# A six-layer decoder on one core: keys and values of the last attention moved into the experts' stage, the fp8 layer moved into the last attention's round

## The reference

```
x = x + L0_attn (layernorm(x))        # self attention, 16 heads of 64, rotary, causal
x = x + L0_xattn(layernorm(x), ctx)   # cross attention, 16 heads of 32, causal
x = x + L0_ffn  (layernorm(x))        # 32 experts, each takes its 8 best tokens
x = x + L1_attn (layernorm(x))        # q * sum(k * v), q and k of unit length
x = x + L1_xattn(layernorm(x), ctx)   # cross attention, 16 heads of 32, biases
x = x + L1_ffn  (layernorm(x))        # x and weight rounded to e4m3, product, bias
```

## Time and profile before

| | us |
|---|---|
| median of 3 runs (3672.01 to 3676.06) | 3674.29 |
| the profiled execution | 3670.53 |
| its span, first to last instruction | 3668.7 |
| mean granted TensorE clock | 0.926 of full |

### The profile page before, as it was taken

One profiled execution on the slowest core, in us unless ns is written; L12 is line 12 of the kernel. 1 busy time (PEld: TensorE's weight loads), 2 busy tenths in 40 slices (PEclk: granted clock), 3 DMA queues, 4 the chain that ended last, 5 costly groups with the idle time before them and its releaser, 6 DMA issues. The chain is left out here.

```text
span 3668.7 us, 71550 instructions
## 1 busy us (share of the span) xinstructions
PE 3132.1 (85%) x23760; PEld 2321.1 (63%) x23768; DVE 2103.6 (57%) x5235; ACT 1382.7 (38%) x4549; POOL 1312.0 (36%) x1964
## 2 busy tenths in 40 slices
PE   5999999999987999998575666659998899999935
PEld 5888888888865878786321111116776688888822
DVE  6666766667646787886500000016665667666667
ACT  4434434444434555554200000011111566666611
POOL 2544535445433444443100000002222455555537
PEclk9999999999998999999688877779999899999976
DMA  3001000000002211111699999971112111121123
GB/s 124 18 17 34 17 34 17 21 31 17 29 18 88 69 46 57 58 47 51 263 424 424 428 428 426 428 317 59 63 69 80 61 62 46 46 69 46 34 84 132
DMA packets 123955, 438.33 MB, mean 119 GB/s; under 512 B 11056, under 2 KB 30768, under 8 KB 103376
## 3 DMA queue, kind: packets, MB, share of 16 engines
q1 hardware_dynamic: 119792, 433.27, 30.4%
q10 hardware_dynamic: 4096, 4.20, 0.3%
HBM read 390.78 MB, written 46.66 MB: 119 GB/s over the span
## 5 line engine op out<-in xcount | busy, mean ns | idle before, releaser
L405 POOL TENSOR_TENSOR cross_prob<-cross_prob,cross_rsum 128x256 f32<-128x256 f32 (+1 forms) x1024 | 561.4, 576 | 626.5 <-DVE cross_rsum L780 624.9
L643 ACT ACTIVATE cross_prob<-cross_S,cross_neg_max 128x256 f32<-128x256 f32 (+1 forms) x1024 | 446.7, 455 | 93.6 <-DVE cross_neg_max L772 75.2
L405 POOL TENSOR_TENSOR self_prob<-self_prob,self_rsum 128x128 f32<-128x128 f32 (+1 forms) x512 | 285.3, 583 | 243.4 <-DVE self_rsum L780 243.3
L549 PE MATMUL cross_T<-cross_ident,cross_prob 128*128 128x128 f32 x1792 | 294.2, 281 | 25.3 <-ACT cross_probT L650 13.0
L643 ACT ACTIVATE self_prob<-self_S,self_neg_max 128x128 f32<-128x128 f32 (+1 forms) x512 | 212.0, 425 | 202.3 <-DVE self_neg_max L772 202.2
L1164 PE MATMUL experts_H<-moe_w,experts_tok 128*32 128x512 f32 x1024 | 164.9, 802 | 132.8 <-DMA moe_b<-in_L_ffn_w 126.9
L549 PEld LDWEIGHTS cross_T<-cross_ident,cross_prob 128*128 128x128 f32 x1792 | 203.6, 141 | 116.2 <-issue 43.2
L399 POOL TENSOR_TENSOR self_QK_T<-self_QK_T,self_turned 128x512 f32<-128x512 f32 x128 | 164.4, 1284 | 308.4 <-DVE self_QK_T L737 308.3
L785 DVE COPY cross_probT<-cross_T 128x384 f32<-128x384 f32 (+1 forms) x256 | 158.7, 620 | 150.8 <-PE cross_T L549 150.3
L650 ACT ACTIVATE cross_probT<-cross_T 128x384 f32<-128x384 f32 (+1 forms) x256 | 139.8, 546 | 279.2 <-PE cross_T L549 278.2
L1224 DVE COPY experts_hidT<-experts_T 128x512 f32<-128x512 f32 x32 | 22.1, 692 | 371.5 <-PE experts_T L1175 371.5
(11 more groups left out here) (252 smaller groups left out, 9109.0 us busy)
## 6 DMA issues: line engine op xcount, KB each, us to landing
moe_w<-in_L_ffn_w SPq DMA_DIRECT2D x64, 4096.0 KB, 34.7
cross_x_t<-x SPq DMA_DIRECT2D x32, 512.0 KB, 5.5
cross_c_t<-in_ctx SPq DMA_DIRECT2D x32, 512.0 KB, 6.4
cross_res<-x SPq DMA_DIRECT2D x32, 512.0 KB, 3.6
x<-cross_res SPq DMA_DIRECT2D x32, 512.0 KB, 2.8
self_x_t<-in_x SPq DMA_DIRECT2D x16, 512.0 KB, 3.6
self_res<-in_x SPq DMA_DIRECT2D x16, 512.0 KB, 3.6
x<-self_res SPq DMA_DIRECT2D x16, 512.0 KB, 2.8
```

The costliest lines, as they stand in the source:

```text
L405: ins = pool.tensor_tensor(pr, pr, rsum[:, h, t:t + 1].to_broadcast([P, KQ[t]]), ALU.mult)
L549: mm = pe.transpose(TP[:, o:o + P], prob[:, h % NP, SOFF[t] + k * P:SOFF[t] + (k + 1) * P], ident[:, :])
L643: ins = act.activation(prob[:, h % NP, SOFF[t]:SOFF[t] + KQ[t]], SC[h % G][:, SOFF[t]:SOFF[t] + KQ[t]], ACT.Exp, bias=neg_max[:, h, t:t + ...
```

## The change

Four things:

1. **K and V of the last attention move into experts.** In route, SP loads Wk and Wv in eight blocks of 128 rows and ACT and DVE split them beside the routing. In the experts' loop a turn (two experts) also takes one batch: SP loads its context, ACT and DVE split it, PE computes K in two halves and V in two halves, placed after hidden and after output, DVE copies them out (K with its bias), and ACT stores them to `keys_d` and `values_d` in DRAM, 512 KB each. The expert's bias row b1 is loaded as `[4, 512]` instead of `[1, 2048]`, and its product uses a constant `rows` loaded from DRAM instead of a row of ones made by POOL.
2. **One last phase** (`last_phase`) takes the place of cross1 and fp8. It loads K and V of each batch in 4 + 4 pieces, computes Q only, and carries the fp8 layer of the last batch in the same round: F (transposes of the quantised x) and G (products) on PE, fstats, fapply and G on DVE, F on ACT, frstd, fbias and fout on POOL. It has orders of its own.
3. **The fp8 weight** is rounded in norm, five of ten DVE steps in each of the last two batches, and goes through DRAM (512 KB).
4. **Prologues.** In the attention phases each projection waits for its own weight (`weights_for(w, c, n)`) and not for all; the splits of the later weights come after X1, and in self0 part of them after K0. In self0, where V, prob and QK_T serve as staging, the first writes to them wait for the last piece staged there (`staged`).

```diff
     "last": {
         "PE":   "Q2 T15- S1 PV3- T0 Q3 T1 O0- X0+ T2 S2 X1+ T3 O1- T4 Q0+ T5 S3 T6 Q1+ T7 PV0 T8 F0- F1- T9 PV1 T10 S0+ T11 G0- "
                 "T12 G1- T13 PV2 T14"
         "DVE":  "max3 take14- inv1 inv2 z2- stats+ max4 max5 take0 z3- max6 max7 apply+ inv3 inv4 O0- take2 X0+ inv5 max8 max9 "
                 "inv6 X1+ max10 inv7 max11 inv8 inv9 O1- take4 fstats- inv10 max12 take6 max13 fapply- max14 take8 z0 inv11 "
                 "max15 inv12 inv13 inv14 take10 max0+ max1+ max2+ take12 z1 inv15 inv0+ G0- G1-"
         "POOL": "rstd+ norm2 norm3 norm4 norm5 norm6 norm7 norm8 norm9 frstd- res norm10 norm11 norm12 norm13 norm14 fbias- "
                 "norm15 norm0+ fout- norm1+"
...
-            def weights_for(n):
+            def weights_for(w, c, n):
                 if isinstance(n, int) and n == 0:
-                    pe.wait_ge(w_lo, len(PIECES))
+                    pe.wait_ge(w_lo, PIECES.index((w, c)) + 1)
...
-            high_pieces(len(PIECES) - 2)
-            if bq is not None:
-                act.wait_ge(scaled, 1)
-            act.wait_ge(const_in, 16 * N_CONST)
+            high_pieces(1)
...
+                def load_rows(i):
+                    if i >= 3:
+                        sp.wait_ge(kv_lo, i - 2)
+                    sp.dma_start(kv_stage[:, i % 3, :], (wk, wv)[i // KD][i % KD * P:(i % KD + 1) * P, :]).then_inc(kv_in[i], 16)
...
             def _(sp):
+                sp.dma_start(rows[:, :, :], consts["rows"]).then_inc(rows_in, 16)
+                sp.dma_start(bk_c[:, :], bk).then_inc(bk_in, 16)
+                sp.dma_start(c_t[:, :, :], ctxT[0].rearrange("(k p) s -> p k s", p=P)).then_inc(c_in, 16)
                 with sp.Fori(1, E // 2) as i:
+                    sp.wait_ge(c_lo, 2 * i)
+                    sp.dma_start(c_t[:, :, :], ctxT[i].rearrange("(k p) s -> p k s", p=P)).then_inc(c_in, 16)
...
                 with pe.Fori(0, E // 2) as i:
-                    for s in range(2):
-                        hidden(2 * i + s, i, s)
-                        output(2 * i + s, i, s)
+                    hidden(2 * i, i, 0)
+                    pe.wait_ge(c_lo, 2 * i + 2)
+                    keys(i, 0)
+                    output(2 * i, i, 0)
+                    keys(i, 1)
+                    hidden(2 * i + 1, i, 1)
+                    values(i, 0)
+                    output(2 * i + 1, i, 1)
+                    values(i, 1)
...
+                        if s == 0:
+                            act.wait_ge(kv_ok, 4 * i + 4)
+                            act.dma_start(keys_d[bass.ds(i, 1)].rearrange("o g p s -> p (o g) s"), k_sb[:, :, :]).then_inc(k_stored, 16)
+                        else:
+                            act.wait_ge(kv_ok, 4 * i + 6)
+                            act.dma_start(values_d[:, bass.ds(i, 1)].rearrange("g o p t c -> p (g o) t c"), v_sb[:, :, :, :]).then_inc(v_stored, 16)
...
+                def keys_out(i, half):
+                    dve.wait_ge(kv_full, 4 * i + half + 2)
+                    dve.wait_ge(k_stored, 16 * i + 16)
+                    for j in range(2):
+                        g = 2 * half + j
+                        ins = dve.tensor_scalar(k_sb[:, g, :], KV[half][:, j * S:(j + 1) * S], bk_c[:, g:g + 1], None, ALU.add)
+                    ins.then_inc(kv_ok, 1)
...
             def body(n, i, s, last):
                 for u, (which, t) in enumerate(ORDER):
+                    if isinstance(n, int) and u < 5:
+                        quantise(u + 5 * s)
                     dve.wait_ge(p_full, NU * n + u + 1)
```

More of the change, by code:

```diff
@@ L1233, in norm_attention_phase @@
+                tokens(0, 0)
+                with dve.Fori(0, E // 2 - 1) as i:
+                    for s in range(2):
+                        expert(i, s, False)
+                for s in range(2):
+                    expert(E // 2 - 1, s, s == 1)
+def norm_attention_phase(nc, n_batch, x_in, x_out, consts, sel_d, out_d, w2, wq, bq, wk, bk, wv, bv, weight, w8_d):
     E, Q = out_d.shape[2], out_d.shape[1]
@@ new lines, in output @@
+            def output(key, n):
+                t = key[1]
+                pe.wait_ge(z_ok, n * NG + NG)
+                out = bank_for(key, n)
+                if isinstance(n, int) and n == 0:
+                    pe.wait_ge(w_lo, 2)
+                mm = split_products(pe, out[:, :], [((zTs[0][:, k, t * P:(t + 1) * P], zTs[1][:, k, t * P:(t + 1) * P]),
+                                                     (wos[0][:, k, :], wos[1][:, k, :])) for k in range(NG)])
+                full(mm, key, n)
@@ new lines, in linear_transposes @@
+            def linear_transposes(key, n):
+                pe.wait_ge(fl, NF * n + NF)
+                if isinstance(n, int) and n == 0:
+                    pe.wait_ge(w8_in, 32)
+                out = bank_for(key, n)[:, 0:S].bitcast(BF16)
+                for kk in range(2):
+                    for t in range(T):
+                        k = 2 * key[1] + kk
+                        mm = pe.transpose(out[:, (kk * T + t) * P:(kk * T + t + 1) * P], xb[:, t, k * P:(k + 1) * P], ident_b[:, :])
+                full(mm, key, n)
@@ new lines, in linear, with scores @@
+            def linear(key, n):
+                t = key[1]
+                taken(n, [("F", 0), ("F", 1)])
+                out = bank_for(key, n)
+                for k in range(KD):
+                    mm = pe.matmul(out[:, :], x8T[:, k, t * P:(t + 1) * P], w8[:, k, :], start=(k == 0), stop=(k == KD - 1))
+                full(mm, key, n)
+            def scores(n, g, off):
+                taken(n, [("Q", g)])
+                pe.wait_ge(keys_in[g], n * 16 + 16)
+                after(pe, exp_ok, n, H, G * g, off)
+                for t in range(T):
+                    for i in range(G):
+                        r = i * d_head
+                        mm = pe.matmul(SC[i][:, t * S:(t + 1) * S], QT[r:r + d_head, g, t * P:(t + 1) * P], KT[r:r + d_head, g, :],
+                                       start=True, stop=True, tile_position=(r, 0))
+                        if t == T - 1:
+                            mm.then_inc(s_full, 1)
@@ new lines, in exps, with take @@
+            def exps(n, h, off):
+                act.wait_ge(max_ok, n * H + h + 1)
+                after(act, t_full, n, H, h - NP + 1, off)
+                for t in range(T):
+                    ins = act.activation(prob[:, h % NP, t * S:(t + 1) * S], SC[h % G][:, t * S:(t + 1) * S], ACT.Exp,
+                                         bias=neg_max[:, h, t:t + 1], scale=1.0, accum_out=sums[:, h, t:t + 1])
+                ins.then_inc(exp_ok, 1)
+            def take(n, h, off):
+                act.wait_ge(t_full, n * H + h + 1)
+                after(act, pv_ok, n, H, h - NPT + 1, off)
+                act.activation(probT[:, h % NPT, :], TP[:, :], ACT.Copy).then_inc(pt_act, 1)
@@ L1641, in constants @@
+            over_batches(dve, n_batch, body)
 def constants():
@@ L1716, in decoder @@
     norm1(x2, x4)
-    cross1(x4, x5)
-    fp8(x5, out)
+    last(x4, out)
 def kernel(**inputs):
```

750 lines of the change are left out of this document (571 added, 179 removed), and 6 rows, old and new, of the table ORDERS.

## The result

| | before | after |
|---|---|---|
| median of four runs, us | 3673.15 (3671.62 to 3676.06) | 3515.68 (3510.41 to 3519.17) |
| ratio, with its interval | | 0.9569 (0.9553 to 0.9586) |
| span of the profiled execution | 3668.7 | 3513.9 |

What follows compares the result with a forecast made beforehand. PE bounds cross1, DMA the experts; no fp8 engine is full. 3668.7 - 121.6 - 151.7 + 13.8 - 11 - 17 + 3 + 72 + 6 = 3462 us span, median 3468; 3430 to 3510 (chance 0.64), wider range 3425 to 3550.

Steps and rivals of the forecast that it cites:

- The bound of each stage: PE's issue bounds cross1 and the norm stage, DMA engines bound the experts; the joined round can't be under PE's 31.0 us.
- The last stage's round: Joined attention and fp8 round: PE's need of 31.0 and 1.3 us, 32.3 against 39.9, sixteen batches giving -121.6 us.
- Hidden, unless a load misses its group: Last stage: SP's K, V, x, res and result transfers, 2.6 MB in 32 us, cost nothing unless late next round.
- the 1.3 us of slack: Last stage's round over PE's need, judged beside cross0, where PE at 36.85 sets the round within 0.75 us.
- The quantising beside a busy POOL: Last stage's TENSOR_SCALAR on DVE: median 1472 ns, about 1.15 us by the skill's rule; DVE's term up to 1.9 us too high.
- Rival A: Last stage: DVE bounds the joined round, keeping 7.4 us of waits beside 29.4 of work: 36.8 us, 3540 total; chance 0.18.
- B: Experts: K's store takes 42 us where 36 are free, DVE and PE wait: +5.6 us per pair, 3552; chance 0.07.
- C: Experts: each row of K's store waits for two w1 rows, 80 us, a pair of 89, run near 4130; chance 0.04.
- D: Experts: PE isn't hidden, at half clock a pair is 57 us, 3650 in total; chance 0.03.
- The experts: K and V moved there: a pair from 40.7 to 44.9 us, 15 times +63, start 6, end 3.2; sum +72 (55 to 85).
- The bias row's -0.5: Experts: w1's bias as four rows on four partitions relieves one late DMA engine, -0.5 us per pair.
- self0's start: Prologue of self0: first Q and K products overlap the remaining weight pieces, -12 us (0 to -20).

Runs made afterwards that it cites:

- the two experiments: Changes to after's experts: K of each batch stored a second time, 3531.3 us; K and V from one product instead of three, 3519.1 us.
- the two ways: Against after: SyncE loads res as soon as O1's copy has read the old one, 3502.8 us; or POOL adds res behind norm14, 3492.0 us.
- the addition in the next round: After with res loaded early, its bias added by POOL in the next round behind norm2, and experts' constants loaded in routing: 3472.5 us.
- g_on_act: The kernel of res_both with the two copies of the fp8 product (G0, G1) moved from DVE to ACT: 3501.2 us, ratio 0.9536.
- res_both: After with res loaded as soon as O1's copy is done and its bias added by POOL between norm10 and norm11: 3499.0 us, ratio 0.9528.
- the second store: After with K of each batch in the experts stored a second time by ACT to spare DRAM, 0.52 MB more per pair: 3531.3 us, ratio 0.9614.
- the exchange of its form: The kernel adding res behind norm2, with epsilon's addition as a TENSOR_TENSOR with a constant tile instead of a TENSOR_SCALAR: 3472.1 us, ratio 0.9457.

## Why the prediction was right or wrong

**The bound of each stage: right.** DMA in the experts (share 1.02, 425 GB/s, and the two experiments), PE in norm. In the last stage PE's work is the bound only once the other two things are out of its way.

**The last stage's round: the step that failed.** The sum took PE's need and 1.3 us, 32.3, and the round was 35.4: 16 x 3.1 = 49 us, the whole miss. That the result is in the range all the same is the range's width: the forecast kept rounds of 31 to 36 open without naming what would fill them. The rest of that stage came as said: the first product 14.9 us after its start (14 forecast), and what is left beside the rounds 614.8 - 16 x 35.4 = 48 us against 50 in the sum. Two clauses of the prediction carried the mistake. "Hidden, unless a load misses its group": the K and V loads were hidden (2.1 us to landing), but `res` missed, and the prediction, which put such a miss at nothing, never asked where SP issues it (behind S3) and where POOL stands for it (ahead of norm10). Landing in 3.6 us from DRAM it could not be there. Removing it in the two ways gave 0.65 and 1.9 us of the 3.1, the addition in the next round 2.4. The other: the 1.3 us of slack came from cross0, where POOL was idle 21 of 37.6 us; here it is idle 8.2 of 35.3. DVE's sum, 29.4 against 30.2, came out by luck: it held 1.47 us for each quantising operation, which took 0.62 in this kernel (1.7 us too much a round), and nothing for the stretch of epsilon's addition (2.3 us too little).

**The quantising beside a busy POOL: half right.** The prediction weighed whether the quantising would take 1.47 us or some 1.15 beside a busy POOL, and read it as a question of DVE's volume. Measured: 0.54 with POOL idle, 1.14 and 1.50 beside it (1.27 on average; the estimate by the rule of the Trainium skill was 1.15). But its price isn't volume: a DVE lighter by 1.27 us gained nothing, while twice 0.73 us of stretch ahead of xb, with 1.0 of epsilon's, came with a round 2.4 us longer, and twice 0.49 ahead of the next x with the shortest round of all. It also missed that a 128x2 operation is stretched like a large one, by 2.3 us a round.

**Rival A** (a full DVE, 36.8) named a round close to the measured one (35.4) for another reason; g_on_act excludes it in the kernel of res_both. **B and C** didn't come: K's 16 stores landed after these times, not after 42 to 80 us.

```profile
DMA to landing us min/median/max: 12.7/13.5/23.8
```

The packets of several descriptors of the Trainium skill (DMA: Bandwidth & Descriptors, "Queues, rings and completion order"), by which the store takes two to four turns, fit that; a turn itself isn't shown by any row. **D** didn't either: 502.55 of 650 us, granted clock 0.90 against 0.79 in the earlier trace rows.

**The experts: right, by two errors that partly cancel.** A pair went from 40.7 to 44.3, +3.6 where +4.2 was said. Its 1.57 MB cost 3 x 1.1 = 3.3 us by the second store (3.6 against the mean of the stage), nearest to the 3.7 at 420 GB/s: 4.7, from the fp8 stage's rows, was the wrong neighbour, since a share read in a half empty stage isn't what a full queue takes. The bias row's -0.5 was nothing. The start was said to cost 6 us and cost 8.7: hidden(0) came 9.7 us after the stage began instead of 1.0, for `bk_c` on DVE besides `rows`. Taking that wait away gave 2.6 back, because the context is next in the queue.

**Routing** +8.2 (ACT stood 4.4 us for the fourth block of Wk at 1781.8, as forecast), **norm** +3.9: right.

**self0's start: too high.** 12 us were counted, some 5 came (4.5 and 8 by single pairs of executions). The first product came 23.6 us earlier, at 14.93, and gave little, because V is written last:

```profile
41.46 2.29 DVE L713 TENSOR_TENSOR self_wol<-self_V,self_woh 128x2048 fp32r<-128x2048 f32 x1 [5.13 <-ACT self_woh L614]
43.86 1.29 DVE L759 COPY self_V<-self_A 128x512 f32<-128x512 f32 x2
...
44.60 0.58 PE L73 MATMUL self_A<-self_xTh,self_wqh 128*128 128x256 f32 x1 [10.93 <-DVE self_V L759]
```

The last weight piece is staged in V; its load, high part and low part end at 43.8, and both PSUM banks hold V products that wait for it, PE 10.9 us behind them. The prediction named this staging and priced it too low.

## What to carry on

When two phases are merged, list every load's three times: when its buffer is free, where in the issuing engine's order it stands, and what the engine that consumes it does next. A wait of 4 us on an engine at 77% was worth 2 us of every round.

Before an idle gap is filled, look at what runs beside it: POOL's gap was free for POOL and not for DVE. DVE's operations that read two SBUF operands, or copy and scale within SBUF, are to be placed where POOL waits, whatever their size, if a chain hangs on them; where nothing hangs on them, as on the normalising of the next x here, POOL may work beside them.

## What the runs showed of the hardware

A TENSOR_SCALAR of 128x2 values that takes 0.17 us took 3.08 in a steady round of after, from 3131.34 to 3134.42. POOL issued four instructions back to back there, the last ending at 3134.40:

```profile
3130.98 2.27 POOL L1819 TENSOR_TENSOR last_y<-last_y 128x512 f32<-128x512 f32 x2
...
3131.34 3.08 DVE L2069 TENSOR_SCALAR last_rstd<-last_mv 128x2 f32<-128x2 f32 x1
3133.21 1.19 POOL L1796 TENSOR_TENSOR last_prob<-last_prob,last_rsum 128x256 f32<-128x256 f32 x2
```

So it didn't get in between two of them, while the quantising one did (1.14 and 1.50 us beside additions of 1.3). Under which condition it does is open; no run was made for it. Whether the 1.4 us that this operation still takes in the fastest kernel cost anything wasn't tried either: the exchange of its form left them there.
